# One transfer per weight piece: a partition holds neighbouring weight rows in an adapter kernel with three roles

## What is computed

```python
h = einsum('bsh,bhk->bsk', x, W_down[role]) + b_down[role]      # 1024 -> 512
h = gelu(h, approximate=False)
u = einsum('bsk,bkh->bsh', h, W_up[role]) + b_up[role]          # 512 -> 1024
y = x + u
mean, var = mean and variance of y over its last axis
out = (y - mean) * rsqrt(var + 1e-5) * gamma[role] + beta[role]
```

## Time and profile before

| | |
|---|---|
| median of three runs | 1418.1 us |
| the profiled execution | 1418.03 us |
| its span (first to last event on the engines) | 1416.3 us |
| TensorE matmul busy | 1401.5 us, 99% |
| TensorE weight load busy | 1158.7 us, 82% |
| VectorE busy | 1207.1 us, 85% |
| ScalarE busy | 778.0 us, 55% |
| GpSimd busy | 200.9 us, 14%, in two stretches |
| granted TensorE clock | 0.998 of full speed (2.4 GHz) |
| DMA | 283.49 MB, 200 GB/s on average |

### The profile page before, as it was taken

How to read it: one execution, slowest core, us unless ns; L and a number is a source line. 1 busy time by engine, 2 the same in 40 slices (tenths; PEclk the granted TensorE clock), 3 DMA queues, 4 the chain that set the end, 5 groups by cost and what they waited for, 6 DMA issues and landing times.

```text
span 1416.3 us, 29328 instructions
## 1 busy us (share of the span) xinstructions
PE 1401.5 (99%) x6175; PEld 1158.7 (82%) x6176; DVE 1207.1 (85%) x1456; ACT 778.0 (55%) x2053; POOL 200.9 (14%) x300
## 2 busy tenths in 40 slices
PE   8999999999999999999999999999999999999997
PEld 6888888888888888888888888888888888888886
DVE  7799988888888888888888899988888888888887
ACT  5555555555555555555555555555555555555555
POOL 3377311100000000000000377311100000000000
PEclk9999999999999999999999999999999999999999
DMA  9678777766666656666666778767766666666664
GB/s 228 184 227 236 210 218 199 212 195 200 184 194 198 194 183 196 198 193 185 194 199 192 215 227 230 225 199 211 207 197 185 200 199 186 185 195 201 189 186 149
DMA packets 208868, 283.49 MB, mean 200 GB/s; under 512 B 25791, under 2 KB 155584, under 8 KB 208846
## 3 DMA queue, kind: packets, MB, share of 16 engines
q1 hardware_dynamic: 201870, 269.60, 62.3%
q0 software_dynamic: 5888, 12.07, 5.0%
q10 hardware_dynamic: 1088, 1.57, 0.4%
HBM read 183.27 MB, written 99.88 MB: 200 GB/s over the span
## 4 chain that ended last, share of the span: by engine, by line
PE 97%; DVE 1%; DMA 1%; ACT 0%; issue 0%; DVEq 0%; ACTq 0%
PE p_down L1077 16%; PE p_up L1079 16%; PE p_down L1079 16%; PE p_up L1077 16%; PE p_down L1078 16%; PE p_up L1078 16%; DMA row<-in_L_cond_W_down 0%; DMA x_quad<-in_x 0%; DVE row L997 0%; PE p_hT L1073 0%; DMA w_raw<-in_itok_B 0%; DVE row L794 0%; DVE wd_lo L732 0%; DVE row L840 0%; ACT wd_hi L548 0%
## 5 line engine op out<-in xcount | busy, mean ns | idle before, releaser
L1077 PE MATMUL p_down<-wd_hi,xT_hi 128*128 x1012 | 393.9, 389 | 1.1 <-DVE wd_lo L732 0.6
L1079 PE MATMUL p_down<-wd_hi,xT_lo 128*128 x1012 | 393.7, 389 | 0.0
L1078 PE MATMUL p_down<-wd_lo,xT_hi 128*128 x1012 | 393.7, 389 | 0.0
L1077 PE MATMUL p_up<-wu_hi,hT_hi 128*128 x1008 | 392.3, 389 | 0.0
L1079 PE MATMUL p_up<-wu_hi,hT_lo 128*128 x1008 | 392.1, 389 | 0.0
L1078 PE MATMUL p_up<-wu_lo,hT_hi 128*128 x1008 | 392.1, 389 | 0.0
L585 ACT ACTIVATE hT_hi<-p_hT 128x512 fp32r<-128x512 f32 x126 | 75.5, 599 | 382.0 <-DVE p_hT L774 379.8
L794 DVE SCALAR_TENSOR_TENSOR row<-p_up,row 128x1024 f32<-128x1024 f32 x126 | 154.1, 1223 | 125.5 <-PE p_up L1079 125.5
L571 ACT ACTIVATE xT_hi<-xT_raw 128x1024 fp32r<-128x1024 f32 x125 | 132.7, 1062 | 187.7 <-PE p_down L1079 185.5
L1077 PEld LDWEIGHTS p_down<-wd_hi,xT_hi 128*128 128x128 f32 x1012 | 189.9, 188 | 40.8 <-issue 1.8
L1079 PEld LDWEIGHTS p_down<-wd_hi,xT_lo 128*128 128x128 f32 x1012 | 190.2, 188 | 39.6
(11 more groups left out here) (174 smaller groups left out, 982.8 us busy)
## 6 DMA issues: line engine op xcount, KB each, us to landing
x_quad<-in_x SPq DMA_DIRECT2D x510, 128.0 KB, 3.5
row<-in_x SPq DMA_DIRECT2D x126, 512.0 KB, 4.1
out<-row SPq DMA_DIRECT2D x126, 512.0 KB, 2.7
h_dram<-h SPq DMA_DIRECT2D x125, 256.0 KB, 4.1
h_quad<-h_dram SPq DMA_DIRECT2D x500, 64.0 KB, 2.0
w_raw<-in_L_cond_W_down POOLq DMA_DIRECT2D x64, 64.0 KB, 3.2
w_raw<-in_L_cond_W_up POOLq DMA_DIRECT2D x64, 64.0 KB, 3.8
row<-in_L_cond_W_up SPq DMA_DIRECT2D x16, 128.0 KB, 4.2
```

Of the source, the lines that this page charges most:

```text
L1077: pe.matmul(dst, a_hi, w_hi, start=first, stop=False)
L1078: pe.matmul(dst, a_hi, w_lo, start=False, stop=False)
L1079: return pe.matmul(dst, a_lo, w_hi, start=False, stop=last)
```

## The change

The order of the contraction changes. Partition p now holds the neighbouring rows 8p to 8p+7 of `W_down` (chunk c is row 8p+c) and 4p to 4p+3 of `W_up`. A piece is then one pattern of HBM and comes by one transfer with 128 partitions: those of the first role, and those that GpSimd loads. A partition's part of a first `W_down` piece is 4 KB in one run, where it was two runs of 2 KB.

To agree with that, VectorE's block transposes read x with 8 elements (32 bytes) between neighbours, and h with 4 elements (16 bytes), where they read neighbours without a gap; the number of elements and what is written stay. `bias_h` of the first three sequences writes with 128 elements between neighbours.

In the queues: ScalarE issues pieces 0 and 1 as its first two instructions, and rounds piece 0 before it waits for the sort and issues its two x transfers; it issues nothing of piece 2. SyncE issues all of piece 2 (one transfer) and piece 3 (one) where it issued two and four.

```diff
-        wd_view = W_down.rearrange("r (q c a) k -> r q a c k", q=NQ, a=BLK)
-        wu_view = W_up.rearrange("r (q c a) h -> r q a c h", q=NQ, a=BLK)
+        wd_view = W_down.rearrange("r (p c) k -> r p c k", c=HC)
+        wu_view = W_up.rearrange("r (p c) h -> r p c h", c=KC)
...
-            for q in quads:
-                if n < FD:
-                    w = FC // K
-                    dst = buf[BLK * q:BLK * q + BLK, 0:FC].rearrange("p (c k) -> p c k", c=w)
-                    eng.dma_start(dst, wd_view[R - 1, q, :, n * w:n * w + w, :]).then_inc(first_raw[n], 16)
+            if n < FD:
+                w = FC // K
+                eng.dma_start(buf[:, 0:FC].rearrange("p (c k) -> p c k", c=w), wd_view[R - 1, :, n * w:n * w + w, :]).then_inc(
+                    first_raw[n], 16)
...
-            load_first(sp, FD - 2, range(NQ // 2, NQ))
+            load_first(sp, FD - 2)
             load_first(sp, FD - 1)
...
-                        for q in range(NQ):
-                            src = wd_view[bass.ds(r, 1), q, :, bass.ds(2 * m + par, 1), :].rearrange("o a c k -> (o a) (c k)")
-                            pool.dma_start(w_raw[par][BLK * q:BLK * q + BLK, :], src).then_inc(pool_raw[par], 16)
+                        src = wd_view[bass.ds(r, 1), :, bass.ds(2 * m + par, 1), :].rearrange("o p c k -> (o p) (c k)")
+                        pool.dma_start(w_raw[par][:, :], src).then_inc(pool_raw[par], 16)
...
-            load_first(act, 0, range(0, 1))
+            load_first(act, 0)
+            load_first(act, 1)
             act.wait_ge(out_ready, 1)
             act.activation(factor[:, 0:1], opener[:, 2:3], ACT.Gelu)
-            load_first(act, 0, range(1, NQ))
-            load_first(act, 1)
...
+            round_first(0)
             act.wait_ge(first_known, 1)
             load_quads(act, act.value_load(first_numbers[0:1, 0:1], min_val=0, max_val=B - 1), 0, range(NQ // 2, NQ))
...
-            round_first(0)
             act.wait_ge(order_in_psum, 1)
...
             round_half(0, 0)
-            load_first(act, FD - 2, range(0, NQ // 2))
...
             def turn_x(raw, par, c):
                 return (raw.rearrange("p c (g t) -> p g c t", g=NQ),
-                        x_quad[par][:, :, c * BLK:c * BLK + raw.shape[1] * BLK].rearrange("p g (c a) -> p g c a", a=BLK))
+                        x_quad[par][:, :, :].rearrange("p g (a c) -> p g c a", c=HC)[:, :, c:c + raw.shape[1], :])
...
                 dve.transpose(p_hT[:, :].rearrange("p (c g t) -> p g c t", c=KC, g=NQ),
-                              h_quad[:, :, :].rearrange("p g (c a) -> p g c a", a=BLK)).then_inc(h_transposed, 1)
+                              h_quad[:, :, :].rearrange("p g (a c) -> p g c a", c=KC)).then_inc(h_transposed, 1)
...
-                    by_chunk = dict(q=NQ, c=KC, a=BLK)
-                    dve.tensor_tensor(h[:, :].rearrange("p (c q a) -> p q c a", **by_chunk),
-                                      src.rearrange("p (q c a) -> p q c a", **by_chunk),
-                                      bias.rearrange("p (q c a) -> p q c a", **by_chunk), ALU.add).then_inc(biased, 1)
+                    dve.tensor_tensor(h[:, :].rearrange("p (c j) -> p j c", c=KC),
+                                      src.rearrange("p (j c) -> p j c", c=KC),
+                                      bias.rearrange("p (j c) -> p j c", c=KC), ALU.add).then_inc(biased, 1)
```

More of the change, by code:

```diff
@@ L491, in _ @@
                     pool.wait_ge(slot_free, 2)
-                raw0 = (part - 1) * (DN // 2 + UN // 2) * 64
+                raw0 = (part - 1) * (DN // 2 + UN // 2) * 16
                 split0 = (part - 1) * (DN + UN)
@@ L495, in _ @@
                     for par in range(2):
-                        for q in range(NQ):
-                            src = wd_view[bass.ds(r, 1), q, :, bass.ds(2 * m + par, 1), :].rearrange("o a c k -> (o a) (c k)")
-                            pool.dma_start(w_raw[par][BLK * q:BLK * q + BLK, :], src).then_inc(pool_raw[par], 16)
+                        src = wd_view[bass.ds(r, 1), :, bass.ds(2 * m + par, 1), :].rearrange("o p c k -> (o p) (c k)")
+                        pool.dma_start(w_raw[par][:, :], src).then_inc(pool_raw[par], 16)
                     for par in range(2):
-                        split_piece(par, raw0 + 64 * m + 64, split0 + 2 * m + par + 1, wd_hi, wd_lo,
+                        split_piece(par, raw0 + 16 * m + 16, split0 + 2 * m + par + 1, wd_hi, wd_lo,
                                     weights_at + 2 * PC * m + PC * par)
                     pool.wait_ge(pieces_split, split0 + 2 * m + 3)
-                raw0 += DN // 2 * 64
+                raw0 += DN // 2 * 16
                 split0 += DN
@@ L506, in _ @@
                     for par in range(2):
[L507 to L510, removed]
+                        src = wu_view[bass.ds(r, 1), :, bass.ds(m, 1), PC * par:PC * par + PC].rearrange("o p c h -> (o p) (c h)")
+                        pool.dma_start(w_raw[par][:, :], src).then_inc(pool_raw[par], 16)
                     for par in range(2):
-                        split_piece(par, raw0 + 64 * m + 64, split0 + 2 * m + par + 1, wu_hi, wu_lo,
+                        split_piece(par, raw0 + 16 * m + 16, split0 + 2 * m + par + 1, wu_hi, wu_lo,
                                     weights_at + 2 * PC * m + PC * par)
@@ L526, in first_piece, with round_first @@
             buf = row[n % RING][:, 0:FC]
-            count = 16 * NQ
             if n < FD:
-                return buf, wd_hi[:, n * FC:n * FC + FC], wd_lo[:, n * FC:n * FC + FC], count
+                return buf, wd_hi[:, n * FC:n * FC + FC], wd_lo[:, n * FC:n * FC + FC]
             m = n - FD
-            return buf, wu_hi[:, m * FC:m * FC + FC], wu_lo[:, m * FC:m * FC + FC], count
+            return buf, wu_hi[:, m * FC:m * FC + FC], wu_lo[:, m * FC:m * FC + FC]
         @block.scalar
         def _(act):
-            load_first(act, 0, range(0, 1))
+            load_first(act, 0)
+            load_first(act, 1)
             act.wait_ge(out_ready, 1)
             act.activation(factor[:, 0:1], opener[:, 2:3], ACT.Gelu)
-            load_first(act, 0, range(1, NQ))
-            load_first(act, 1)
+            def round_first(n):
+                buf, hi, lo = first_piece(n)
+                act.wait_ge(first_raw[n], 16)
+                act.activation(hi, buf, ACT.Copy).then_inc(first_hi, 1)
+            round_first(0)
             act.wait_ge(first_known, 1)
             load_quads(act, act.value_load(first_numbers[0:1, 0:1], min_val=0, max_val=B - 1), 0, range(NQ // 2, NQ))
-            def round_first(n):
-                buf, hi, lo, count = first_piece(n)
-                act.wait_ge(first_raw[n], count)
-                act.activation(hi, buf, ACT.Copy).then_inc(first_hi, 1)
             def copy_param(n, src, at, size, loaded):
```

14 lines of the change are left out of this document (6 added, 8 removed).

## The result

| | before | after |
|---|---|---|
| median | 1418.15 us (1417.81 to 1419.1, 4 runs) | 1455.97 us (1453.17 to 1457.81, 4 runs) |
| the profiled execution, and its span | 1418.03, 1416.3 us | 1455.07, 1453.3 us |
| granted TensorE clock | 0.998 | 0.998 |

After to before is 1.0264 (1.0251 to 1.0277): 37.8 us slower, where 1417.4 us was forecast. The range ended at 1426.0 and does not hold it.

What follows compares the result with a forecast made beforehand. TensorE's unbroken stream of some 6,060 matmuls was taken as the bound, with only the start shortenable: 1418.03 - 0.76 (hole closed) + 0.1 (queue order) = 1417.4 us, other terms nothing; range 1416.5 to 1426.0.

Steps and rivals of the forecast that it cites:

- VectorE's strided reads: Block transposes of x and h: gapped reads add nothing; upper bound 1.43 us for a sequence (0.95 x, 0.48 h).
- the margin: Quiet stretch, `sum_y` to `subtract_h` on VectorE: 1.03 us can be added per sequence before TensorE waits.
- Rival 1: Strided reads halve the transposes' rate, TensorE waits 0.40 us per sequence: 50 us, up to 17 more, say 1475; chance 0.10.
- Its mild form: Only x slowed, by 0.95 us; loss only in GpSimd's stretches, 3 to 15 us, say 1424 us; chance 0.07.
- The start, the transfers: First products: piece 2 of `W_down` lands at 14.2 us, closing TensorE's hole; gain 0.76 us.
- The start, the queue order: ScalarE rounds piece 0 before issuing its x transfers, delaying the first product; cost taken as 0.1 us.
- Rival 3: The start gains nothing: x held up (1418.6 us) or piece 2 lands no earlier than 15.95 (1418.1 us); chance 0.10.
- GpSimd's loads: GpSimd's rounds of two pieces: issue takes 1.1 us instead of 4.0, a round about 10.6 us instead of 13.15; gain 0.
- Rival 2: GpSimd's denser rounds make VectorE late beside them: 2.6 us, 1420 us, or 1424 if in step; chance 0.07.
- The gapped bias: Bias writes of the first sequences, three instructions on VectorE: 0.48 us more each, hidden behind products.

Runs made afterwards that it cites:

- the gaps gone: Kernel after, with both block transposes reading neighbours without a gap, single transfers and new queue order kept (mismatched rows): 1417.85 us, ratio 0.9998.
- the place changed: Kernel after, with the x transpose moved behind `subtract_h` and `write_out` ahead of it, both transposes still reading with gaps: 1429.42 us, ratio 1.0071.
- one part alone: Two kernels: the kernel after with only x, or only h, read with gaps and the other as before: 1425.98 us and 1419.63 us.
- the five doses: Five kernels by us added between `sum_y` and `subtract_h`: only h gapped 0.37, x transpose moved 0.41, only x gapped 0.91, the change 1.27, extra gapless transposes 1.47.
- early dose: Kernel before, with two extra gapless half transposes on VectorE in each sequence, between `sum_y` and `subtract_h`: 1483.8 us, ratio 1.0471.
- The kernel with reads at several distances: Kernel after, with steady transposes reading x and h at distances of 1, 2, 4 and 8 elements in turn (mismatched rows): 1431.32 us, one run.

## Why the prediction was wrong, point by point

**The step that failed** is "VectorE's strided reads": "I take nothing: an element takes one step of this engine in every row of that size, whatever the number of operands, so the reading of one operand isn't what paces it". All rows of that size read without a gap, so they say nothing of gaps. The row picked as the nearest, the bias in runs of 32 elements, has none inside a run. The two reads added 1.30 us, close to the upper bound of 1.43. The prediction had that bound, its margin and its consequence written out, and set them at a chance of 0.10 against "only the lack of a row". Lack of a row is no argument for zero; where one of two bounds lies beyond the margin, and nothing on record chooses between them, the chance of crossing deserved far more than 0.10.

The Trainium skill was on the other side, and it was right. Its page "Advanced Engine Details and Errata", section "Memory Cachelines", asks for at least two hits on each SBUF line of 16 bytes. The distances agree: 8 bytes cost nothing (1202 ns), 16 bytes cost 1982. The Trainium skill gives no factor; measured, from 16 bytes on, it is 1.62 to 1.77 for the 1024 elements of x and 1.46 to 1.60 for the 512 of h.

**Rival 1**, the full form, is what happened: its mechanism, its place and its margin. The chain is shown by undoing each link: the gaps gone (1417.85 us), the place changed (884 matmuls), one part alone (883 and 884), the delay made without gaps (0.43 us for 1.47). Its size was 50 us plus up to 17 and was 37.0 between the profiled executions:
- It took 0.40 us for a sequence by 1.43 - 1.03; measured are 1.30 by the means and 1.27 in the row, hence 0.24 to 0.27, and 0.26 by the count. The term that was too large is the price of an element: 0.371 us for the 512 of h, not 0.48. For x, 0.928 for 0.95 forecast.
- 0.26 x 125 = 33 us.
- The start, 32.13 against 30.36 us for the up product of sequence 0, is 1.8 us.
- Beside GpSimd, in 845 to 1045 us, 857 matmuls start where the quiet rate gives 864: 1.6 us. In 45 to 145 us none are missing beyond the quiet rate. The 17 us that were added as possible there did not come. Two things may have spared them, and no run tells them apart: VectorE beside GpSimd was stretched less than before (below), and a sequence of 11.12 us leaves it 0.26 us more.
- 33 + 1.8 + 1.6 = 36 of the 37.0 us; the last one is not placed.

**Its mild form** stood as "only x is slowed": 3 to 15 us, 1424. With x alone it measured 1425.98; of the 10.0 us of its profiled execution 7.0 are lost in GpSimd's stretches, as said, and 1.1 at the start. It isn't the case of this change, since h is slowed too.

**The margin**, 5.44 - 0.29 - 3.88 - 0.24 = 1.03 us, is the number that held best: the five doses put the corner between 0.91 and 1.27, and both points beyond it lie on it within 0.02 us. That it fits the mean so well is partly luck. The sequence of rows 9 and 10 is the tightest of the four of a round. In the kernel after, in the quiet stretch, `sum_y` starts 0.29 us behind the up product in one sequence of four and 0.20 in the other three, and TensorE starts 0.24 us behind `subtract_h` in two of four and 0.15 in the other two. That is a margin of 1.16 us on average, and makes the first matmul 0.14 us late; but where TensorE has had to wait, its second matmul comes 0.10 us late on top of it, a term the prediction doesn't have. Together 0.24 us, and 0.42 by the same reading in the early dose. The kernel with reads at several distances has a case in between, both reads at 16 bytes:

```profile
422.19 1.22 DVE L805 SCALAR_TENSOR_TENSOR row<-p_up,row 128x1024 f32<-128x1024 f32 x1 [1.11 <-PE p_up L1089]
...
426.55 0.66 DVE L791 TENSOR_TENSOR hT_lo<-p_hT,hT_hi 128x512 fp32r<-128x512 f32 x1
```
```profile
427.20 0.39 PE L1089 MATMUL p_down<-wd_hi,xT_lo 128*128 x1
427.43 0.42 PE L1087 MATMUL p_up<-wu_hi,hT_hi 128*128 x1
427.69 0.39 PE L1088 MATMUL p_up<-wu_lo,hT_hi 128*128 x1
```

The stretch is 426.55 + 0.66 - 422.19 = 5.02 us, 1.14 more than 3.88, over the 1.03 by 0.11. TensorE loses 0.03, at the second matmul alone. So the 1.03 is the margin of the tightest sequence, and a good mean only with the 0.10 that it leaves out.

**The start, the transfers.** Piece 2 was to land at 14.2 and the hole of 0.76 to close. It landed at 14.66 in the kernel after and at 15.02 without gaps, just inside the 15.1 that was allowed, and without gaps the hole closed. That piece 3's chunk "is in time" failed there: piece 3 landed at about 17.5, 7.9 us after its issue, where a transfer of that size had 4.1 at the median. Why it took so long no run tells. The gain went into the next hole; the working had priced piece 3's subtraction, and not its landing. In the kernel after the start is worse for another reason: its six half transposes take 1148 ns instead of 710 and delay what follows them. TensorE in order of time:

```profile
12.76 0.49 PE L1068 MATMUL p_down<-wd_hi,xT_hi 128*128 x1 [0.45 <-DVE xT_lo L748]
...
16.60 0.49 PE L1068 MATMUL p_up<-wd_hi,hT_hi 128*128 x1 [0.85 <-issue]
...
19.24 0.39 PE L1070 MATMUL p_up<-wd_hi,hT_lo 128*128 x1
19.88 0.49 PE L1068 MATMUL p_down<-wd_hi,xT_hi 128*128 x1 [0.24 <-DVE wd_lo L724]
```

**The start, the queue order.** Taken at 0.1 us, bounds below nothing and 0.26 or one rounding. ScalarE and its queue in order of time, kernel after:

```profile
0.84 0.89 ACTq L266 DMA_DIRECT2D row<-in_L_cond_W_down  x2
...
5.18 1.06 ACT L538 ACTIVATE wd_hi<-row 128x1024 fp32r<-128x1024 f32 x1 [1.92 <-DMA row<-in_L_cond_W_down]
6.11 0.88 ACTq L275 DMA_DIRECT2D x_quad<-in_x  x2
```

Piece 0 was rounded from 5.18 (5.10 without gaps), later than the bound of 4.95, and the x transfers left 0.5 us later than the 5.62 of before. The number was fetched beside the rounding, from 5.2 us, so the rounding's 1.07 us did not come on top. Without gaps this cost nothing: VectorE's first transpose of x started at 9.63, right behind a subtraction of its own and without a wait for x (9.81 before), and the first product at 12.01 instead of 12.19. In the kernel after it did cost something: VectorE waited 0.41 us for x and began that transpose at 9.98, 0.17 later than before, and the gaps made it 0.40 longer; the first product came at 12.76, 0.57 later. The forecast of 0.1 is right in size. Its landing time for piece 0 was not, and that the first product hangs on the last x transfer was too strong: VectorE's own work ended at the same time.

**Rival 3**, the start gains nothing (1418.1 to 1418.6), is true of the transfers as such: 0.9998 without gaps. By a mechanism it didn't name, the next piece.

**GpSimd's loads.** Two issues for a round, 562 ns each, 1.1 us: as forecast. GpSimd in order of time without gaps, first copies of the first two rounds:

```profile
58.52 0.61 POOL L465 CAST wd_hi<-w_raw 128x512 f32 x1 [3.96 <-DMA w_raw<-in_L_cond_W_down]
...
69.78 0.62 POOL L465 CAST wd_hi<-w_raw 128x512 f32 x1 [4.82 <-DMA w_raw<-in_L_cond_W_down]
```

This round took 11.26 us, where it was 13.15, and the landing is in view, with waits of 4.0 and 4.8 us. Over the eight rounds of this stretch, whose first copies start from 58.52 to 131.97, a round took 10.5 us on average, for 10.6 forecast; before it was 12.8 (59.52 to 149.36). The gain was 0, as said.

**Rival 2**, denser rounds make VectorE late, had the wrong sign. In 83 to 94 us VectorE is busy 9.19 of 11 us without gaps, where it was 10.90; but GpSimd is busy 5.68 us there and was 9.22. From 45 to 145 us VectorE is busy 85.39 us, where it was 91.22. Over the whole span it is 1194.9 against 1207.1 us, the same instructions. GpSimd's `wd_lo` took 1389 ns on average, for 1798 before. Why fewer and larger transfers leave VectorE less stretched is open: that GpSimd's instructions happen to fall beside others of VectorE fits as well, and no run tells them apart.

**The gapped bias** was to take 0.48 us more and be hidden; it took 1106 for 684 ns, 0.42 more, in three instructions. One of them was not hidden in the kernel after. From 23.96 to 25.08 us it stands on the chain that ended last, between the split of the turned h and ScalarE's copy, after which TensorE starts at 25.80 behind a hole of 25.80 - 25.20 - 0.227 = 0.37 us. The hole is smaller than the 0.42; but the transposes before it had delayed it as well, and no run separates the two. Without gaps in the transposes there is no hole at this place.

## What to carry to other kernels

Before changing a layout, look at the distance between neighbouring fp32 elements on VectorE's side of it: in SBUF 8 bytes were free and 16 bytes or more made a block transpose take 1.5 to 1.8 times as long, reading or writing, while PSUM as a destination was free. Put the time into the stretch between the wait for TensorE and the result that TensorE waits for, not into VectorE's total: of 1.30 us added there, about 1.0 were free and the rest was paid in each sequence, and moving the same work behind that stretch gave 27 of 38 us back. A price without a row in the profile goes in at its bounds, and where the bounds straddle the margin the chance goes there too.

## What the runs showed of the hardware

- The step at 16 bytes between fp32 elements, and that it is a step: 1204, 1202, 1982, 2127, 1947 and 2061 ns for 1024 elements read at 4, 8, 16, 32, 64 and 128 bytes. Writes into SBUF: 1205, 1982, 2121 and 2077 ns at 8, 16, 32 and 128. Into PSUM 726 to 727 ns for 512 at 8 to 64 bytes.
- Why 32 bytes cost more than 16, 64 or 128 is open; no run here looks into it.
- TensorE, once held up by a late operand, loses 0.10 us more at its second matmul: 0.33 us between the first two instead of 0.227, in every sequence of the quiet stretch of the kernel after.
- At the start a transfer of 512 KB issued 0.46 us behind another of the same size landed 7.9 us after its issue, the one ahead of it 5.9 (about 6.4 and 5.6 in the kernel after), while in the steady state one took 4.1 us at the median.
- One issue by GpSimd over 128 partitions costs 562 ns, one over 32 partitions 503: a quarter of the transfers took 28% of the issue time.
